# Scan: POOL makes five of sixteen products of B and du in place of one of three

## What is computed

```python
def step(hst, inputs):
    ut, dt, bt, ct = inputs
    dA = jnp.exp(dt[..., None] * A)
    hst = hst * dA + (dt * ut)[..., None] * bt[:, :, None, :]
    y = jnp.einsum('bkdn,bkn->bkd', hst, ct)
    return (hst, y)
```

## Time and profile before

| | |
|---|---|
| runs | 28426.21, 28437.24, 28440.13 us; median 28437.24 us |
| profiled execution | span 28422.8 us from first to last instruction; its own time isn't given apart from the span |
| DVE busy | 25435.4 us, 89% of the span |
| PE busy | 23013.8 us, 81% |
| POOL busy | 22836.6 us, 80% |
| ACT busy | 14594.8 us, 51% |
| mean granted TensorE clock | 0.839 of full speed |
| DMA | 2332.84 MB, mean 82 GB/s |

### The profile page before, as it was taken

The page is one execution under the profiler, slowest core; times in us unless marked ns, Lnnn a source line. Parts: engine busy times, 40 slices in busy tenths (PEclk is TensorE's granted clock), DMA queues, the critical chain, the costliest instruction groups (busy, mean ns, idle before and its releaser), DMA issues. The chain is left out here.

```text
span 28422.8 us, 328026 instructions
## 1 busy us (share of the span) xinstructions
PE 23013.8 (81%) x97488; PEld 6745.8 (24%) x97488; DVE 25435.4 (89%) x16259; ACT 14594.8 (51%) x20067; POOL 22836.6 (80%) x10240
## 2 busy tenths in 40 slices
PE   8888888888576888888887888888875888888885
PEld 3322222222232222222233222222212322222222
DVE  3489999999579999999986999999997899999997
ACT  1255555555266555555514655555552655555552
POOL 0169999999036999999981799999990499999992
PEclk9978888888766888888868888888887888888887
DMA  2242222121454222212266422122226622222224
GB/s 86 97 138 45 49 49 49 40 48 41 157 187 160 49 49 49 47 41 49 49 218 218 130 49 49 42 46 49 49 58 216 203 48 49 49 45 43 49 49 146
DMA packets 1121174, 2332.84 MB, mean 82 GB/s; under 512 B 98406, under 2 KB 609347, under 8 KB 1110717
## 3 DMA queue, kind: packets, MB, share of 16 engines
q1 hardware_dynamic: 1117572, 2308.66, 29.8%
q10 hardware_dynamic: 1728, 1.70, 0.0%
HBM read 1329.40 MB, written 980.58 MB: 81 GB/s over the span
## 5 line engine op out<-in xcount | busy, mean ns | idle before, releaser
L1589 POOL TENSOR_TENSOR scan_hc<-scan_bc,scan_h 128x1024 f32<-128x1024 f32 x6912 | 16065.4, 2354 | 116.6 <-DVE scan_h L1766 115.7
L1766 DVE TENSOR_TENSOR_SCAN scan_h<-scan_da,scan_state,scan_dbu 128x1024 f32<-128x1024 f32 x6912 | 15989.1, 2338 | 141.4 <-ACT scan_da L1643 135.4
L1680 PE MATMUL scan_da<-scan_dd,scan_ssel 32*128 32x512 f32 x27648 | 9115.9, 746 | 3002.1 <-DVE scan_h L1766 2768.0
L1643 ACT ACTIVATE scan_da<-scan_da,scan_a_cur 128x1024 f32<-128x1024 f32 x6912 | 7516.2, 1087 | 7740.0 <-PE scan_da L1680 7734.7
L1680 PE MATMUL scan_p_du<-scan_dd,scan_ssel 32*128 32x512 f32 x27648 | 9207.7, 745 | 449.2 <-DVE scan_dbu L1753 170.8
L1753 DVE TENSOR_TENSOR scan_dbu<-scan_p_du,scan_bc 128x1024 f32<-128x1024 f32 x4608 | 5561.5, 1207 | 375.3 <-PE scan_p_du L1680 336.6
L1575 POOL TENSOR_TENSOR scan_dbu<-scan_bc,scan_dus 128x1024 f32<-128x1024 f32 x2304 | 5427.2, 2356 | 58.6 <-ACT scan_dus L1617 57.5
L1680 PEld LDWEIGHTS scan_da<-scan_dd,scan_ssel 32*128 32x128 f32 x27648 | 2456.7, 217 | 10300.7 <-DVE scan_h L1766 8724.7
L1697 PE MATMUL scan_p_y<-scan_hc,scan_rsel 128*32 128x512 f32 x27648 | 4781.9, 773 | 20.7 <-POOL scan_hc L1589 20.6
L1680 PEld LDWEIGHTS scan_p_du<-scan_dd,scan_ssel 32*128 32x128 f32 x27648 | 2416.3, 212 | 3522.1 <-DVE scan_dbu L1753 2947.5
L1622 ACT ACTIVATE scan_state<-scan_h,scan_a_cur 128x1 f32<-128x1 f32 x6912 | 2023.5, 293 | 1575.4 <-DVE scan_h L1766 1465.2
(11 more groups left out here) (225 smaller groups left out, 13400.7 us busy)
## 6 DMA issues: line engine op xcount, KB each, us to landing
scan_bc<-bc_d SPq DMA_DIRECT2D x576, 512.0 KB, 12.0
du_d<-prep_useq SPq DMA_DIRECT2D x384, 576.0 KB, 3.7
delta_d<-prep_delta SPq DMA_DIRECT2D x384, 576.0 KB, 4.6
y_d<-scan_y SPq DMA_DIRECT2D x576, 384.0 KB, 5.2
scan_dd<-delta_d SPq DMA_DIRECT2D x1136, 192.0 KB, 4.8
scan_dd<-du_d SPq DMA_DIRECT2D x1136, 192.0 KB, 6.5
fin_y<-y_d SPq DMA_DIRECT2D x288, 576.0 KB, 5.6
xs_d<-proj_xs_o SPq DMA_DIRECT2D x96, 588.0 KB, 3.3
```

The costliest lines, as they stand in the source:

```text
L1589: nc.gpsimd.tensor_tensor(hc[:, u % HC_SLOTS, :], c, h[:, u % H_SLOTS, :], ALU.mult).then_inc(hc_ready, 1)
L1643: nc.scalar.activation(da[u % DELTA_BANKS][:], da[u % DELTA_BANKS][:], ACT.Exp, scale=a_cur[:, slot(u)[0], u % UNITS:u % UNITS + 1]).then_ ...
L1680: return nc.tensor.matmul(dst[:, half * H:(half + 1) * H], ssel[rows, i, :], dd[rows, s, m, j, :], start=True, stop=True)
L1766: nc.vector.tensor_tensor_scan(h[:, v % H_SLOTS, :], da[v % DELTA_BANKS][:], dbu[:, v % DBU_SLOTS, :], state[:, v % UNITS:v % UNITS + 1], ...
```

## The change

The fixed third (`TRIO` = 3) goes. Units are taken in turns of 16, of which units 2, 5, 8, 11 and 14 (`SHARED`) are POOL's, and the other eleven are DVE's own; unit 15 of a turn was every third time POOL's before and now is never. The distance between two shared units is 3 inside a turn and 4 from the last of a turn to the first of the next, so `after(u)` replaces u + 3, and `shares(u)` (the number of shared units ahead of u) replaces u // 3 in the counts that the semaphores wait for. A round has 60 shared units and 132 own ones, in place of 64 and 128. POOL still makes a shared product four units ahead (`SHARE_AHEAD`). PE waits for the next chunk's loads at the last shared unit of a chunk (unit 46 of 48) in place of unit 47.

```diff
-TRIO = 3
+TURN = 16
+SHARED = (2, 5, 8, 11, 14)
+ROUND_SHARES = ROUND // TURN * len(SHARED)
+ROUND_OWN = ROUND - ROUND_SHARES
+SHARE_AHEAD = 4
...
 def shared(u):
 
-    return u % TRIO == 2
+    return u % TURN in SHARED
+
+
+def shares(u):
+
+    return len(SHARED) * (u // TURN) + sum(s < u % TURN for s in SHARED)
+
+
+def after(u):
+
+    return next(v for v in range(u + 1, u + TURN) if shared(v))
...
                 def rounds(r, last):
                     q = r * ROUND
                     for u in range(ROUND):
-                        ahead = u + TRIO + 1
+                        ahead = u + SHARE_AHEAD
                         if shared(ahead) and not (last and ahead >= ROUND):
                             share(r, ahead)
...
                 def rounds(r, first, last):
                     q = r * ROUND
                     for u in range(ROUND):
-                        if shared(u) and not (last and u + TRIO >= ROUND):
-                            copy_share(r, u + TRIO)
+                        if shared(u) and not (last and after(u) >= ROUND):
+                            copy_share(r, after(u))
...
-                        if u % UNITS == UNITS - 1 and not (last and u == ROUND - 1):
-
-                            s, n = slot(u + TRIO)
+                        if shared(u) and after(u) // UNITS > u // UNITS and not (last and after(u) >= ROUND):
+
+                            s, n = slot(after(u))
                             t.wait_ge(loaded[s], r * (TURNS * LOADS) + n * LOADS + ONE)
...
-                        t.wait_ge(dbu_ready, r * (ROUND // TRIO * 2) + (u // TRIO * 2 + u % TRIO) + ONE)
+                        t.wait_ge(dbu_ready, r * ROUND_OWN + (u - shares(u)) + ONE)
                         if not shared(u):
 
-                            t.wait_ge(share_copied, r * (ROUND // TRIO) + (u // TRIO + 1) + ONE)
+                            t.wait_ge(share_copied, r * ROUND_SHARES + (min(shares(u) + 1, ROUND_SHARES) if last else shares(u) + 1) + ONE)
                             spread(p_du, 1, u, 0)
                             spread(p_du, 1, u, 1).then_inc(du_spread, 1)
-                        elif not (last and u + TRIO >= ROUND):
-                            spread_share(r, u + TRIO)
+                        elif not (last and after(u) >= ROUND):
+                            spread_share(r, after(u))
...
```

More of the change, by code:

```diff
@@ L1507, in scan @@
         FIRST_UNITS = EIGHT
+        FIRST_SHARE = next(u for u in range(FIRST_UNITS) if shared(u) and after(u) >= FIRST_UNITS)
         FIRST_LOADS = (2 * 2 * 2 + 2) * 16
@@ L1569, in share @@
                 def share(r, u):
-                    g.wait_ge(share_copied, r * (ROUND // TRIO) + (u // TRIO + 1) + ONE)
+                    g.wait_ge(share_copied, r * ROUND_SHARES + (shares(u) + 1) + ONE)
                     g.wait_ge(scanned, nth(r * ROUND, u - DBU_SLOTS + 1) + ONE)
@@ L1575, in share @@
                     nc.gpsimd.tensor_tensor(dbu[:, u % DBU_SLOTS, :], bc[:, s, image(u % UNITS), :],
-                                            dus[:, u // TRIO % DUS_SLOTS, :], ALU.mult).then_inc(share_ready, 1)
+                                            dus[:, shares(u) % DUS_SLOTS, :], ALU.mult).then_inc(share_ready, 1)
                 def rounds(r, last):
@@ L1594, in _ @@
                 g.memset(state[:], 0.0).then_inc(zeroed, 1)
-                for u in range(TRIO):
-                    if shared(u):
-                        share(0, u)
+                share(0, SHARED[0])
                 rounds(0, False)
@@ L1613, in copy_share @@
                 def copy_share(r, u):
-                    a.wait_ge(share_spread, r * (ROUND // TRIO) + (u // TRIO + 1) + ONE)
-                    a.wait_ge(share_ready, nth(r * (ROUND // TRIO), u // TRIO - DUS_SLOTS + 1) + ONE)
-                    nc.scalar.activation(dus[:, u // TRIO % DUS_SLOTS, :], p_du[:], ACT.Copy).then_inc(share_copied, 1)
+                    a.wait_ge(share_spread, r * ROUND_SHARES + (shares(u) + 1) + ONE)
+                    a.wait_ge(share_ready, nth(r * ROUND_SHARES, shares(u) - DUS_SLOTS + 1) + ONE)
+                    nc.scalar.activation(dus[:, shares(u) % DUS_SLOTS, :], p_du[:], ACT.Copy).then_inc(share_copied, 1)
                 def keep(r, u):
@@ L1662, in _ @@
                 a.wait_ge(zeroed, 1 + ONE)
-                for u in range(TRIO):
-                    if shared(u):
-                        copy_share(0, u)
+                copy_share(0, SHARED[0])
                 rounds(0, True, False)
@@ L1704, in rounds @@
                     for u in range(ROUND):
-                        if u % UNITS == UNITS - 1 and not (last and u == ROUND - 1):
-                            s, n = slot(u + TRIO)
+                        if shared(u) and after(u) // UNITS > u // UNITS and not (last and after(u) >= ROUND):
+                            s, n = slot(after(u))
                             t.wait_ge(loaded[s], r * (TURNS * LOADS) + n * LOADS + ONE)
-                        if first and u == FIRST_UNITS - TRIO:
+                        if first and u == FIRST_SHARE:
                             t.wait_ge(loaded[0], LOADS + ONE)
-                        t.wait_ge(dbu_ready, r * (ROUND // TRIO * 2) + (u // TRIO * 2 + u % TRIO) + ONE)
+                        t.wait_ge(dbu_ready, r * ROUND_OWN + (u - shares(u)) + ONE)
                         if not shared(u):
-                            t.wait_ge(share_copied, r * (ROUND // TRIO) + (u // TRIO + 1) + ONE)
+                            t.wait_ge(share_copied, r * ROUND_SHARES + (min(shares(u) + 1, ROUND_SHARES) if last else shares(u) + 1) + ONE)
                             spread(p_du, 1, u, 0)
                             spread(p_du, 1, u, 1).then_inc(du_spread, 1)
-                        elif not (last and u + TRIO >= ROUND):
-                            spread_share(r, u + TRIO)
+                        elif not (last and after(u) >= ROUND):
+                            spread_share(r, after(u))
                         if u % PAIR == 1 and (u >= SUM_LAG or not first):
@@ L1730, in _ @@
                 t.wait_ge(first_loaded, FIRST_LOADS + ONE)
-                for u in range(TRIO):
-                    if shared(u):
-                        spread_share(0, u)
+                spread_share(0, SHARED[0])
                 rounds(0, True, False)
@@ L1749, in times_b @@
                         d.wait_ge(loaded[s], r * (TURNS * LOADS) + n * LOADS + ONE)
-                    d.wait_ge(du_spread, r * (ROUND // TRIO * 2) + (u // TRIO * 2 + u % TRIO + 1) + ONE)
+                    d.wait_ge(du_spread, r * ROUND_OWN + (u - shares(u) + 1) + ONE)
                     d.wait_ge(scanned, nth(r * ROUND, u - DBU_SLOTS + 1) + ONE)
@@ L1759, in recur @@
                     if shared(u):
-                        d.wait_ge(share_ready, r * (ROUND // TRIO) + (u // TRIO + 1) + ONE)
+                        d.wait_ge(share_ready, r * ROUND_SHARES + (shares(u) + 1) + ONE)
                     else:
-                        d.wait_ge(dbu_ready, r * (ROUND // TRIO * 2) + (u // TRIO * 2 + u % TRIO + 1) + ONE)
+                        d.wait_ge(dbu_ready, r * ROUND_OWN + (u - shares(u) + 1) + ONE)
                     d.wait_ge(kept, nth(r * ROUND, u - H_SLOTS + 1) + ONE)
```

## The result

The changed kernel takes 28835.77 us (median of 4 runs, 28784.07 to 28860.39) against 28434.79 us before (4 runs, 28426.21 to 28440.13). The ratio is 1.014, 95% interval 1.0128 to 1.0152: slower by 1.4%, where 0.75% was forecast and the range ended at 28775 us. The profiled execution has a span of 28814.7 us, 391.9 more than before, and a mean granted clock of 0.825 (0.839 before).

A forecast was written before the change was run, and what follows sets the result against it. The prediction took the ring of PE, ACT and DVE, led by DVE, as the bound. Products 161 us, minus 27 at loop edges, plus 78 for clock falls, made +212 us: 28649 us, range 28500 to 28775.

The forecast's parts named there:

- The ring of PE, ACT and DVE: In the scan, these three engines set the pace, with DVE leading and POOL following close behind.
- POOL's 333 us: Scan work POOL sheds, 144 products of 2.31 us; costed at nothing because POOL only follows.
- the products: 144 products of B and du moved from POOL to DVE, 1.12 us each: 161 us added on the path.
- the edges: At 24 loop edges DVE makes its added product while it would have stood waiting: 27 us of 161 cost nothing.
- Copies: ACT makes 144 fewer copies of du; worth nothing, since ACT idles much of the time.
- the earlier wait for loads: PE waits for a chunk's loads one unit sooner, at unit 46 of 48; costed at nothing.
- More falls of the clock: One more fall of PE's clock at each of 432 runs of three own units: 78 us added.
- the mean price: DVE's waiting per clock fall, averaged over the first layer's scan: 0.18 us, used for the added falls.
- my dear one: Upper price of a clock fall, from the two worst falls seen: 0.41 us each, 177 us for 432.
- All is absorbed: Rival: the added products' cost goes into DVE's 472 us of idle time; no change, within 57 us; chance 0.09.
- The clock falls dearly: Rival: each run of three own units brings a fall at the dear price, +311 us, 28748 us; chance 0.14.
- POOL is the bound: Rival: POOL's products with C hold DVE's scans, so shedding them gains 333 us, 28104 us; chance 0.11.

The follow-up runs named there:

- quarter_busy256: Changed kernel with POOL given four of sixteen units, plus four unread filling matmuls on PE at each even unit: 28515.0 us, ratio 1.0032 against the kernel before.
- five16_busy256: Changed kernel plus four unread filling matmuls on PE at each even unit: 28057.34 us, ratio 0.987 against the kernel before.
- quarter: Changed kernel with POOL given four of sixteen units (2 and 6 of 8), no filling matmuls: 29348.87 us, ratio 1.0328 against the kernel before.
- run12: Changed kernel with turns of 12, units 2, 5, 8 and 10 POOL's; product counts of the kernel before: 29487.57 us, ratio 1.0372 against that kernel.
- five16_clumped: Changed kernel with units 2, 4, 7, 10 and 12 of a turn on POOL, same counts: 29782.57 us, ratio 1.0471 against the kernel before.
- the filled kernel: Kernel before the change plus four unread filling matmuls on PE at each even unit: 28371.46 us, ratio 0.9979 against the kernel before.

## Why the prediction was wrong in size and right in direction

**Right: what bounds the kernel.** The ring of PE, ACT and DVE set the pace, and POOL followed, though only just: it was busy 4981.01 of 5000 us. POOL's 333 us bought nothing, and its wait grew from 115.7 to 789.6 us (about 660 was said, for a smaller loss).

**Right: the products.** 161 us on the path; a product measured at least 1.06 us by itself (`quarter_busy256` against `five16_busy256`), and 1.12 was taken.

**Right: the edges,** 1.24 us by the rows of one, and 1.12 was taken. Around all 24, DVE's idle time in the traces fell from 131 to 104 us, the 27 us of the sum. Copies and the earlier wait for loads cost nothing that the accounting leaves room for.

**Wrong: "More falls of the clock".** The step put one fall more at each of 432 runs of three, at the mean price of 0.18 us, 78 us in all. The accounting above gives about 263 us. The mechanism was right, and so, in the main, was the place; what failed is the mean price, and with it the size.

The clock's record in the two traces shows it. The table counts the falls within the four scans; the kernel before has no runs of three, and its falls are taken at the same units for comparison. A short fall is one of 3.41 us as in the earlier trace rows, a longer one lasts two such stretches or more. What a fall costs is taken as DVE's idle time from its start to the start of the next, without the loop's edges and the first 20 us of a scan.

| falls in the scans | before | changed |
|---|---|---|
| all | 1405 | 1498 |
| time at the lower level | 5852 us | 6877 us |
| short: number, DVE idle, each | 1183, 194 us, 0.16 us | 1125, 197 us, 0.17 us |
| longer: number, DVE idle, each | 222, 101 us, 0.46 us | 373, 351 us, 0.94 us |
| beginning behind a run (between the starts of DVE's scans of units 0 and 3 of a turn of 16): number, DVE idle | 180, 39 us | 386, 221 us |
| of these longer: number, DVE idle | 31, 17 us | 186, 214 us |

*The place.* The run of three is units 15, 0 and 1, and the scan of unit 0 comes right behind its last product. There the falls rise by 206, not by 432; everywhere else they become fewer by 113. Behind the runs lie 182 of the 253 us by which DVE's idle time after falls has grown. That PE is sparse in own units, as the step says, is not what sets the place alone: its gaps lie at the even units, own and shared (see above).

*The price.* A short fall costs as much as before, about the 0.18 us that was taken. But the falls behind the runs are to a large part longer ones, 186 of 386, and these cost 1.15 us each, over six times the mean price and nearly three times my dear one of 0.41. Nearly all of the growth, 250 of 253 us, lies in the longer falls. So the mean over the falls of the kernel before, most of them short, was the wrong price for the falls of a new order.

The other orders fit. The longer falls are 507 in `quarter`, 528 in `run12` and 489 in `five16_clumped`, and 441 of 596, 1068 of 1346 and 1056 of 1475 us of DVE's idle time after falls stand behind them. A short fall is not made dear by coming close behind another, as the short stretches above might suggest: those that begin within 4 us of the end of the last one cost 0.10 us each in the kernel before and 0.16 in the changed one.

**The rivals.** "All is absorbed": no; the accounting leaves none of the 161 us beyond the edges. "The clock falls dearly" came nearest, with a fall at each run and a higher price; it had too many falls and still too low a price. "POOL is the bound" is false for the kernel before as it stands, and true once the clock is held: then POOL is busy 4999.65 of 5000 us, DVE waits for it, and moving products away pays 314 us. The rule of the Trainium skill (Perfetto Trace Analysis, "Identifying the Most-Contended Engine") to work on the engine of highest occupancy first, read from the stretches of the earlier trace rows, failed here: the change that lightens POOL made the kernel 1.4% slower. It holds in the filled kernel, where POOL has no gap left and DVE waits for it.

**Open.** Why a run of three own units is followed by longer falls, and why one order keeps the clock low longer than another, was not derived. Not tested: how an order lies against PE's sums, which are made at odd units alone, while a turn of 16 has its runs always at the same ones.

## What to carry to other kernels

An engine that is busy nearly all the time is the bound only if others wait for it; look for it among the releasers before moving its work. Where PE's clock falls during a stage that two other engines pace, see what holding the clock gives, if need be with matmuls that nobody reads, and try more than one place for them; then balance the others. Don't price one more disturbance by the mean of those already there: look whether the new ones last as long.

## What was not expected of the hardware

More PE work made the kernel faster: four small matmuls at every second unit raised the clock in the scan from 0.84 to 0.99 and took the changed kernel from 28835.77 to 28057.34 us. The place matters: at own units alone, five of eight places, they gave 28142.33 us, at shared units alone, three of eight, 29859.7. DVE lost time mostly to the falls that lasted longer than 3.41 us, 0.94 us each in the changed kernel against 0.17 for a short one. And the order of work on DVE and POOL, at equal counts, moved PE's clock from 0.87 to 0.80 and the time by 3.7%.
